# Two offset-and-resample layers: more store buffers, another hand-over of blends, and the last near source by sums in PSUM

## The reference

```
center, step, prob = w_center.f, relu(w_step.f), sigmoid(w_prob.f)      # per pixel
offset = center * step
th = min(round(row + offset0), 399); tw = min(round(col + offset1), 399)
tgt = mod(int(th*400 + tw), 160000)
sample = grid.at[tgt].set(grid)          # scatter of coordinates: the last source of a target wins
sampled = bilinear sample of f at sample (rounding of the coordinates makes a few rows and columns blend)
proped = sampled*prob + f*(1-prob);  out = f*prob + proped*(1-prob)
```

## Time and profile before

| | us |
|---|---|
| three runs | 9839.02, 9847.34, 9898.68 |
| median | 9847.34 |
| the profiled execution, its own time | 9910.58 |
| its span (first to last instruction) | 9909.0 |
| TensorE busy in it | 6574.7 (66%) |
| VectorE busy | 5644.5 (57%) |
| GpSimd busy | 4705.3 (47%) |
| ScalarE busy | 3752.4 (38%) |

### The profile page before, as it was taken

One profiled execution on the slowest core, in us unless ns is written; L12 is line 12 of the kernel. 1 busy time (PEld: TensorE's weight loads), 2 busy tenths in 40 slices (PEclk: granted clock), 3 DMA queues, 4 the chain that ended last, 5 costly groups with the idle time before them and its releaser, 6 DMA issues. The chain is left out here.

```text
span 9909.0 us, 89353 instructions
## 1 busy us (share of the span) xinstructions
PE 6574.7 (66%) x24132; PEld 2834.2 (29%) x24132; DVE 5644.5 (57%) x11270; ACT 3752.4 (38%) x7426; POOL 4705.3 (47%) x8499
## 2 busy tenths in 40 slices
PE   5666455556623677766777578467777674787888
PEld 2222122222211333332333223223333231333333
DVE  2221444336832432226899887328999994466666
ACT  3444333332211333332333023235555263654555
POOL 2333774414433023334577143247887353566665
PEclk7888678777866888886788888776777886888888
DMA  3555444655442455555555146466554264666666
GB/s 141 181 194 205 138 158 161 161 187 176 140 91 92 169 203 196 209 197 174 186 184 205 49 152 221 140 195 179 156 159 141 89 187 112 187 209 206 220 205 201
DMA packets 489217, 1673.51 MB, mean 169 GB/s; under 512 B 119580, under 2 KB 140347, under 8 KB 421396
## 3 DMA queue, kind: packets, MB, share of 16 engines
q1 hardware_dynamic: 214092, 827.29, 27.1%
q10 hardware_dynamic: 210152, 764.05, 20.3%
q0 software_dynamic: 64480, 76.57, 4.4%
HBM read 949.99 MB, written 727.71 MB: 169 GB/s over the span
## 5 line engine op out<-in xcount | busy, mean ns | idle before, releaser
L974 POOL TENSOR_TENSOR arena<-arena 128x32 f32<-128x32 f32 (+8 forms) x3197 | 970.4, 344 | 3445.6 <-PE ps L1161 3442.5
L1161 PE MATMUL ps<-arena,w_conv 128*10 128x400 f32 x3200 | 1572.4, 603 | 1172.3 <-ACT arena L1220 923.1
L1130 PE MATMUL ps<-arena,minus 128*128 128x400 f32 x3200 | 1817.3, 655 | 632.2 <-DVE arena L1026 512.8
L1024 DVE TENSOR_TENSOR ps<-ps,arena 128x400 f32<-128x400 f32 x1600 | 926.4, 579 | 2168.5 <-PE ps L1138 1239.9
L1286 ACT ACTIVATE arena<-ps 128x400 f32<-128x400 f32 x1600 | 800.2, 500 | 2592.7 <-PE ps L1124 755.1
L1220 ACT ACTIVATE arena<-ps 10x400 f32<-10x400 f32 x1600 | 776.4, 492 | 2058.5 <-PE ps L1161 1064.7
L1174 PE MATMUL ps<-ident,arena 128*128 128x128 f32 x5000 | 923.0, 334 | 871.7 <-issue 471.7
L1104 POOL DMA_INDIRECT arena<-table,gidx x800 | 1201.6, 1502 | 602.8 <-PE ps L1147 337.2
L983 POOL TENSOR_TENSOR arena<-arena 128x32 f32<-128x32 f32 (+8 forms) x3197 | 1142.1, 403 | 10.9
L1236 ACT ACTIVATE arena<-ps 128x512 f32<-128x512 f32 (+1 forms) x1400 | 733.3, 550 | 1015.7 <-PE ps L1174 745.1
L1138 PEld LDWEIGHTS ps<-ident,arena 100*128 100x128 f32 x6400 | 825.5, 163 | 880.8 <-issue 741.5
(11 more groups left out here) (205 smaller groups left out, 5844.5 us busy)
## 6 DMA issues: line engine op xcount, KB each, us to landing
arena<-x SPq DMA_DIRECT2D x200, 1600.0 KB, 12.2
arena<-table SPq DMA_DIRECT2D x400, 800.0 KB
table<-arena ACTq DMA_DIRECT2D x400, 512.0 KB
y<-arena ACTq DMA_DIRECT2D x100, 1600.0 KB, 13.8
arena<-y SPq DMA_DIRECT2D x100, 1600.0 KB
out<-arena ACTq DMA_DIRECT2D x100, 1600.0 KB
table<-arena ACTq DMA_DIRECT2D x200, 576.0 KB
conv<-arena ACTq DMA_DIRECT2D x800, 31.2 KB
```

Of the source, the lines that this page charges most:

```text
L974: last = E.tensor_tensor(tmp[:, :, at:at + size], cols[:, :, y + to:end + to:step], cols[:, :, y:end:step], ALU.subtract)
L1024: V.tensor_tensor(d, d, g, ALU.mult).then_inc(s_mix, 1)
L1130: nc.tensor.matmul(ps[:, 4 + r % 2, 0:W], minus[:, :], tile(t)[:, r * W:(r + 1) * W], start=True, stop=False)
L1161: nc.tensor.matmul(ps[0:10, 7 - count % CB, 0:size], w_conv[lt][:, :], tile(t)[:, at:at + size], start=True, stop=True).then_inc(s_conv, 1)
```

## The change

It has three parts. (1) `c_out` gets six buffers (the two places in columns, each in partitions 0, 64 and 96), and `t_out` four in the two sweeps that do not mix (the added two lie where rows of the table are loaded when mixing); the semaphores of the loads and stores become shared by all sweeps, with running counts in place of `t // FR + 1`. (2) GpSimd's generator takes its step at the clock `(t + behind + 1) * BROWS + 3`, the same expression by which the next tile's owner is chosen. (3) The last near source: for each pair of image rows, VectorE compares two rows with the offset's number i + 1 and writes the power of two 2^(3i//2 - 126) or zero in bfloat16 into one of 8 small buffers; TensorE adds them all up in two PSUM banks by matmuls with a bfloat16 identity; the exponent of the sum tells the highest i, which VectorE takes out by a shift, a scaling and a rounding. A step has four offsets. `blanks(2)` before the loop becomes `blanks(5)` (the memset of `near` before it goes), and the sparse units get six more blanks at their end.

```diff
+HELD = 4
-        c_out = [part(2 * W, 10) for _ in range(2)]
+        c_out = [again(a, 2 * W, 10, F32, p) for p in (0, 64, 96) for a in gates_at]
+        used[0] += 4 * W
+        t_out += [again(rows_at[0] + BROWS * NFIX + a * T_WORDS, T_WORDS) for a in range(2)]
+        found = [again(hit_at + a * W, 2 * W, NB, BF16).rearrange("p (r w) -> p r w", w=W) for a in range(2 * HELD)]
+                nc.vector.tensor_copy(ident16[:, :], ident[:, :])
...
-                yield from piece(V.memset(near, 0.0))
-                yield from blanks(2)
+                yield from blanks(5)
                 dve.wait_ge(s_halo, (u + 1) * 16 * 6)
-                loop0 = n[0]
-                def compare(i):
-                    j, e = divmod(i, SIDE)
-                    src = halo[:, j + RMAX - R:j + RMAX - R + BROWS, RMAX - R + e:RMAX - R + e + W]
-                    note(V.tensor_scalar(m3(hit[i % 2]), src, float(i + 1), float(i + 1), ALU.is_equal, ALU.mult))
-                compare(0)
-                for i in range(SIDE * SIDE):
-                    dve.wait_ge(s_v, loop0 + 2 * i + 1)
-                    if i + 1 < SIDE * SIDE:
-                        compare(i + 1)
-                    else:
-                        dve.wait_ge(s_v, n[0])
-                    note(V.tensor_tensor(near, near, hit[i % 2], ALU.max))
+                for a in range(BROWS // 2):
+                    for i in range(OFFSETS):
+                        c = a * OFFSETS + i
+                        j, e = divmod(i, SIDE)
+                        if c >= 2 * HELD:
+                            dve.wait_ge(s_joined, j0 + c - 2 * HELD + 1)
+                        src = halo[:, j + RMAX - R + 2 * a:j + RMAX - R + 2 * a + 2, RMAX - R + e:RMAX - R + e + W]
+                        V.tensor_scalar(found[c % (2 * HELD)], src, float(i + 1), 2.0 ** (3 * i // 2 - 126),
+                                        ALU.is_equal, ALU.mult).then_inc(s_found, 1)
+                        born[f"found{c}"] = clock[0]
+                        if i % HELD == HELD - 1 or i == OFFSETS - 1:
+                            yield
                     yield
-                dve.wait_ge(s_v, n[0])
+                    dve.wait_ge(s_joined, j0 + (a + 1) * OFFSETS)
+                    yield from piece(V.tensor_scalar(m3(c0m)[:, 2 * a:2 * a + 2, :].bitcast(I32), ps[0:NB, 0:2, 0:W].bitcast(I32), 23, None,
+                                                     ALU.logical_shift_right), f"joined{a}")
+                yield from piece(V.tensor_scalar(c0m, c0m.bitcast(I32), 2.0 / 3.0, 0.45, ALU.mult, ALU.add))
+                yield from piece(V.tensor_scalar(c0m, c0m, MAGIC, None, ALU.subtract))
+                yield from piece(V.tensor_scalar(near, c0m, MAGIC, None, ALU.add))
...
-                    yield from blanks(BLANKS)
+                    yield from blanks(2 * BLANKS)
...
             def tensor(pe, clock):
+                for a in range(BROWS // 2):
+                    if a:
+                        yield from after(pe, clock, f"joined{a - 1}")
+                    for i in range(OFFSETS):
+                        c = a * OFFSETS + i
+                        while clock[0] <= born[f"found{c}"]:
+                            yield
+                        pe.wait_ge(s_found, j0 + c + 1)
+                        for r in range(2):
+                            last = nc.tensor.matmul(ps[0:NB, r, 0:W], ident16[0:NB, 0:NB], found[c % (2 * HELD)][:, r, :],
+                                                    start=i == 0, stop=i == OFFSETS - 1)
+                        last.then_inc(s_joined, 1)
...
+            TR, CR = 2 if mixing else 4, len(c_out)
...
-                            clock[0] = (t + behind + 2) * BROWS + 2
+                            clock[0] = (t + behind + 1) * BROWS + 3
...
-                        if c % 2 == 0 and nth >= 2:
-                            act.wait_ge(s_cst[nth % 2], nth // 2 * 16)
+                        if c % 2 == 0 and nth >= CR:
+                            act.wait_ge(s_cst[nth % CR], nth // CR * 16)
...
-                        if g == a and nth >= 2:
-                            act.wait_ge(s_tst[nth % 2], nth // 2 * 16)
+                        if g == a and nth >= TR:
+                            act.wait_ge(s_tst[nth % TR], (t0[nth % TR] + nth // TR) * 16)
```

More of the change, by code:

```diff
@@ L194, in build @@
         minus = sb("minus", [128, 128])
+        ident16 = sb("ident16", [128, 128], BF16)
         halves32 = sb("halves32", [38, 128])[32:38, :]
@@ L294, in build @@
         s_gath = [sem(f"s_gath{k}") for k in range(DEPTH // GROUP)]
-        s_tst = [sem(f"s_t_st{k}") for k in range(2)]
-        s_cst = [sem(f"s_c_st{k}") for k in range(2)]
+        s_cst = [sem(f"s_c_st{k}") for k in range(len(c_out))]
         s_lst = sem("s_late_st")
@@ L374, in build @@
         s_gatest = sem("s_gatest")
+        s_found = sem("s_found")
+        s_joined = sem("s_joined")
         steps = {"v": 0}
+        s_fld = [sem(f"s_f_ld{a}") for a in range(4)]
+        s_rld = [sem(f"s_rows_ld{a}") for a in range(3)]
+        s_gld = [sem(f"s_gate_ld{a}") for a in range(3)]
+        s_yst = [sem(f"s_y_st{a}") for a in range(4)]
+        s_tst = [sem(f"s_t_st{a}") for a in range(4)]
+        counts = {"f": [0] * 4, "rows": [0] * 3, "y": [0] * 4, "t": [0] * 4}
         def indices(u):
@@ L397, in indices @@
             mark, born = {}, {}
+            OFFSETS = SIDE * SIDE
+            j0 = sum(SIDES[a // 2] ** 2 * (BROWS // 2) for a in range(u))
             STEPS = 2 * 2 + 15 + 16 * 2 + 1 + 4
@@ L904, in sweep @@
             WB = 1 if mixing else 2
[L905 to L908, removed]
+            TR, CR = 2 if mixing else 4, len(c_out)
+            f0, r0, y0, t0 = (list(counts[name]) for name in ("f", "rows", "y", "t"))
+            for t in range(TILES):
+                counts["f"][t % FR] += 1
+                counts["y"][t % FR] += int(mixing)
+            for n in range(2 * TILES):
+                counts["rows"][n % RR] += int(mixing)
+            for n in range(TILES * len(PIECES)):
+                counts["t"][n % TR] += int(tabling)
             if u_idx is not None:
@@ L936, in loaded @@
             def loaded(eng, t):
-                eng.wait_ge(s_fld[t % FR], (t // FR + 1) * 16)
+                eng.wait_ge(s_fld[t % FR], (f0[t % FR] + t // FR + 1) * 16)
             def px(t):
@@ L965, in blend_columns @@
                 if mixing:
-                    eng.wait_ge(s_yst[t % FR], (t // FR + 1) * 16)
+                    eng.wait_ge(s_yst[t % FR], (y0[t % FR] + t // FR + 1) * 16)
                 else:
@@ L1074, in _ @@
                             else:
-                                sp.wait_ge(s_yst[t % FR], t // FR * 16)
+                                sp.wait_ge(s_yst[t % FR], (y0[t % FR] + t // FR) * 16)
                             alone(sp, "sp")
@@ L1120, in row @@
                         if m % HALF == 0:
[L1121 removed]
+                            pe.wait_ge(s_gld[j % RR], (r0[j % RR] + j // RR + 1) * 16)
                         if m >= GB:
@@ L1250, in evacuate_late @@
                         act.wait_ge(s_tevac, count + 1)
-                        for a in range(2):
-                            act.wait_ge(s_tst[a], ((n * len(PIECES) - 1 - a) // 2 + 1) * 16)
+                        for a in range(TR):
+                            act.wait_ge(s_tst[a], (t0[a] + (t * len(PIECES) - 1 - a) // TR + 1) * 16)
                         act.dma_start(tables[u_tab][LATE[t]].rearrange("(q p) c -> p q c", p=LATECOLS),
@@ L1330, in _ @@
                     if tabling:
-                        n = (u_tab + 1) * TILES
-                        for a in range(2):
-                            act.wait_ge(s_cst[a], n * PAIRS // 2 * 16)
-                            act.wait_ge(s_tst[a], n * len(PIECES) // 2 * 16)
+                        for a in range(CR):
+                            act.wait_ge(s_cst[a], (((u_tab + 1) * TILES * PAIRS - 1 - a) // CR + 1) * 16)
+                        for a in range(TR):
+                            act.wait_ge(s_tst[a], counts["t"][a] * 16)
                         act.wait_ge(s_lst, (u_tab + 1) * len(LATE) * 16)
@@ L1337, in _ @@
                         for a in range(FR):
-                            act.wait_ge(s_yst[a], (TILES - a + FR - 1) // FR * 16)
+                            act.wait_ge(s_yst[a], counts["y"][a] * 16)
         sweep(0, None, 0, None)
```

14 lines of the change are left out of this document (7 added, 7 removed).

## The result

The changed kernel takes 8679.6 us, median of 4 runs (8664.41 to 8695.83), against 9850.69 of the kernel before (9839.02 to 9898.68): a ratio of 0.8803 with a 95% interval of 0.877 to 0.8837. The profiled execution took 8695.83 us with a span of 8694.0.

What follows compares the result with a forecast made beforehand. No engine bounds the whole; each sweep has its own limit. Terms -185 - 110 - 205 - 70 - 180 - 55 + 60 + 0 = -745 us took 9910.6 to 9166, as a median 9110 us; 8-in-10 range 8850 to 9480.

Steps and rivals of the forecast that it cites:

- The store term: ScalarE's waits for stores in sweeps one to four: more buffers give back 185, 110, 205 and 70 us.
- The transfer rival: Transfers take the stalls' place in busy stretches, so stores bring only 240 us: median 9435 us, chance 0.17.
- that in which all waits come back: Rival for all sweeps with store or blend waits: every wait returns in full, median 8547 us, chance 0.05.
- the fourth sweep's 139 us: ScalarE's conv-store waits there: half, 70 us, return because VectorE bounds the comparison loop; bounds 20 and 139.
- The hand-over: VectorE's blend waits for GpSimd's in sweeps three and four: exact hand-over gains 180 and 55 us.
- The joins: TensorE's added matmuls bound the two long offset loops: nothing in the fifth sweep, +60 us in the fourth.
- I take 0.8: TensorE's assumed share of time at 2.4 GHz in the two long offset loops, giving 4.36 us a row in the fifth.
- the prediction's own formula: Fifth sweep's loop: 3.96 us a row at full clock, 7.36 at half, weighted by the share of time at 2.4 GHz.
- the price that the prediction set aside: The Trainium skill's 169 ns per added matmul, not 208: some 60 us less in each long loop.
- The slower rival: In both long offset loops TensorE falls to 1.2 GHz and stays: +1233 us there, median 10270 us, chance 0.03.
- The second sweep's end: The gather of moved pixels starts near tile 34 of 50, not 28, and ends with the sweep or just behind.
- a possible bound of the new loop: Fifth sweep's loop: GpSimd's gather, busy for 627 of 730 us before, as its bound would show the forecast wrong.

Runs made afterwards that it cites:

- e1: Only the added store buffers, with old hand-over and old comparison and maximum, against the kernel before: 8936.8 us, ratio 0.9061.
- e3: Only the last near source by TensorE, with two store buffers and old hand-over, against the kernel before: 10168.95 us, ratio 1.0298.
- e7: The changed kernel with GpSimd's old hand-over clock put back: 9019.1 us, 0.9151 of the kernel before.
- e6: The changed kernel with VectorE's old comparison and maximum in place of TensorE's matmuls: 8690.2 us, 0.8806 of the kernel before.
- e5: The changed kernel with two conv and two table buffers as before: 9689.1 us, 0.983 of the kernel before.
- e9: The changed kernel with TensorE's near-source matmuls only in the fifth sweep, comparison and maximum elsewhere: 8672.9 us, 0.8786 of the kernel before.

## Why the prediction was wrong

**The store term was mis-sized, and it is the step that failed.** The prediction said "I take two thirds of the waits", because 206 to 208 GB/s were the highest rates held in busy stretches and 223 was to be the next limit. e1 shows the waits come back whole in the first, third and fourth sweep, 287, 325 and 155 us for 185, 205 and 70, and by three fifths in the second, 181 for 110: 948 for 570. Of the 470 us by which the profiled execution (8696) came under the sum (9166), this term, by e1, is 378. The rates after are 265 and 280 GB/s over stretches of 580 and 440 us. The means of before were taken over stretches with the stalls in them; they said what the kernel asked for, not what the transfers could give. The trace of the kernel before had the answer at the length of a tile: in the stretch that the prediction gives 208 GB/s, 20 us hold 305 (columns as in the earlier trace rows).

```profile
3913.00:3933.00 20.00, 14.10 (x64) 6.45 (x63) 6.68 (x12) 7.34 (x15) 8.27 (x32) 0.98 0.83 305
```

The transfer rival falls with it, and the one nearest to the result is that in which all waits come back (8547), given 0.05.

**Where the fourth sweep's 139 us went, the reason was wrong too.** I halved them as the loop was bound by VectorE anyway. In the comparison loop, 4720 to 5480 us, stood only 20.6 us of them; the others stood outside it, and all came back.

**The hand-over was right in mechanism and size**: 161 and 46 us alone, for 180 and 55. What I did not see is that its worth depends on where the mark falls. The prediction has the mark of the second sweep move by 52 rows, and takes from it only a later gather; with the old clock it would have cost a stall as in the third (e3, e7). So the parts do not add: alone they give -942, -219 and +290 us, -871 together, and the change gave -1171.

**The joins: TensorE became the bound, as forecast; its clock was taken too low.** Put at +60 us, they cost nothing that can be measured (8679.6 us with them, 8690.2 without). "I take 0.8" was the share of time at 2.4 GHz; the clock of 0.98 and 0.99 in the loops puts it near 1. At that the prediction's own formula gives 3.96 us a row for the fifth, and 3.93 was measured. That they agree so closely is luck: the 0.208 us that I took for a join is too much. Most joins start 0.169 us apart, the price that the prediction set aside, and eight take 1.49 us, not 1.66; the rest of a row then takes 2.44 us, not 2.30, and the two errors cancel. The formula gave -73 and -28 us for the two loops; the fifth sweep gained 66 against e6 in this profile, the fourth lost 30. The base that I compared with was before's loop, 35.6 us a tile with stalls in it; without them VectorE alone does it in 34.5 (e6). The slower rival, TensorE held at 1.2 GHz, did not come up; in e3, with stalls left in the bounding engine, a part of it did (clock 0.89).

**The second sweep's end** came as forecast, "with the sweep or just behind": 75 us behind, which costs 44 us with the rest (e6).

**The sixth sweep** gained 41 us of the 1213 though no instruction of it changed. Over the fourteen profiles it takes 1241 to 1319 us, with no part on or off as the cause; this is scatter, and the prediction had no term for it.

## What to carry to other kernels

A rate read off a stretch with stalls in it is a demand, not a ceiling: before giving back part of a stall's time to bandwidth, look for the highest rate over the length of one tile, and in more than one stage: in the first sweep of the kernel before, no 20 us held over 229 GB/s, and it still went to 265. When an in-order engine waits for a small store, count its buffers by when the stores land, not by their size; a few more then returned the whole wait in three sweeps of four. That the small store is late because a large transfer stands ahead of it on the same queue fits the third sweep, where the y stores take 13.8 us to land (median), but no run put them on different queues; the first sweep has no y store and waited as well. The added buffers also lie in other partitions than the first two, and number and place were not tried apart. And take the parts of a change apart in the company of the others: here one part was worth nothing with the rest, cost 3% alone, and set a trap that another removed.

## What the runs showed of the hardware

The transfers of one core held 280 GB/s for 440 us, where the busy stretches read of before showed 208 at most. TensorE, once its stalls were gone, stayed at 0.98 to 1.00 of 2.4 GHz through whole loops of 700 to 990 us, also when the added matmuls had a matrix of zeros. The joins, matmuls of 400 bfloat16 columns, start 0.169 us apart at that clock (median).

GpSimd's issue of an indirect gather, L1136 in the changed kernel, took 0.94 us (median) while VectorE made comparisons of 800 elements (5790 to 6490 us), and 1.61 us in e6 beside comparisons and maxima of 3200 (5715 to 6440). GpSimd was busy for 343 of 700 us in the one and for 623 of 725 in the other. The prediction had it as a possible bound of the new loop; as the comparisons became small, GpSimd's load fell with them.

And the last sweep, bound by no single engine, tends to be slower when its clock is lower, with the same instructions. e5, then e9, over the whole last sweep, the shortest and the longest of the fourteen (columns as above):

```profile
8446.00:9687.00 1241.00, 1051.60 (x4388) 456.07 (x4388) 835.80 (x1593) 646.16 (x1195) 799.31 (x784) 0.88 0.69 217
```

```profile
7353.00:8671.00 1318.00, 1076.34 (x4387) 463.45 (x4385) 832.12 (x1592) 645.61 (x1193) 787.48 (x782) 0.84 0.63 204
```

TensorE's clock is 0.88 in one and 0.84 in the other for 1241 and 1318 us. Whether the clock sets the time, or stops set both, these runs do not tell; it was not tried apart.
